# Attention over packed keys: the values as stationary operand for pair items and the latents' last four groups, with the even projections moved up and the output's addition ahead of a copy

## The chip, the cores and the metric

The kernel runs on one core of a Trainium2 chip. The metric is the device time of one launch in microseconds (us), as the median of several runs. TensorE does the matmuls; ScalarE, VectorE and GpSimd (POOL in the profile) do the rest; SyncE (SP) issues the loads.

## The reference, cut to what matters

Three stages follow each other on x of 4 batches x 256 rows x 256 columns. The change is in the first, a cross attention from the normed rows of x (the latents) to 4096 context tokens of the batch and the latents themselves, with a mask over the context:

```python
q = ln_lat @ Wq                                   # 16 heads of 64
kv = jnp.concatenate([xn, ln_lat], axis=1) @ Wkv
k, v = jnp.split(kv, 2, axis=-1)
weight = jnp.einsum('bhld,bhnd->bhln', q * scale, k * scale)
weight = jnp.where(full_mask[:, None, None, :], weight, neg)
weight = jax.nn.softmax(weight, axis=-1)
out = jnp.einsum('bhln,bhnd->bhld', weight, v)    # 256 queries, n keys, 64 columns a head
x = x + out.transpose(0, 2, 1, 3).reshape(b, l, heads * dim_head) @ Wout
```

The other two stages (a causal attention and two layers of local attention with a feed forward part) are not touched.

## The kernel before, in words

`cross_stage` (lines 103 to 1021) handles the keys of a batch in **items**. The chunks of 128 keys that the mask leaves are listed on the chip, and an item is `latents` (the 256 latents as keys), `pair` (two listed chunks, 256 keys) or `half` (one chunk, 128 keys). `walk` (line 141) gives each engine the same order: the latents of a batch, its pairs, its half, then the next batch. The softmax is an online one: a running maximum `mstate`, a factor `alpha` for what is summed so far, and the sum `o` of 32 columns groups of 64 values and one sum of weights each (65 columns; `v` carries a column of ones, so that the sum of weights comes out of the same matmul).

An item has 8 **steps** j = 0 to 7, one for each group g of 2 heads x 2 query tiles (4 units u of 128 queries). Each engine writes its own order out by hand in its `body` and waits on semaphores. In step j, TensorE (line 371) does:

- in an even step of pair and half items, the scores of groups j and j + 1 (`scores`, line 269). They are split products in fp32r, and head 0 and head 1 lie on partitions 0 to 63 and 64 to 127, so on two row halves of the array;
- the transposes of the probabilities of group j - 2 (`turn_probs`, line 283), 8 for 256 keys;
- one projection of the item's keys or values, or of the next item's first keys in steps 6 and 7 (`projections`, line 322), into the one bank `proj`;
- the weighted values of group j - 3 (`weighted_values`, line 294), plain f32 matmuls: the turned probabilities `pt` are stationary (128 x 128) and 65 columns of `v` move, 8 matmuls for 256 keys, into the bank `pv_ps`;
- in step 3, the next item's tokens turned (`turn_tokens`, line 246).

Groups 5 to 7 of an item thus have their weighted values in steps 0 to 2 of the next item, and the transposes of 6 and 7 stand in its steps 0 and 1.

VectorE (line 842) does in step j: the addition `o += pv_ps` of group j - 4 (`add_output`, line 814); in step 4 the next tokens times the norm's gain (line 753); the maxima of group j (`maxima`, line 786), which also copy the scores out of PSUM; the copy of half the transposes of j - 2 (`store_turned`, line 806; the other half is ScalarE's, line 514); and then one piece of other work: low parts of keys `kl` (line 766) in steps 0, 4, 6 and 7, statistics of the next tokens in step 0, the normed tokens `z` in step 2, the low part of the turned tokens in step 5, penalties in step 7.

ScalarE (line 539) does the copy of the transposes of j - 2, the copy of the projection (`kh` or `v`), then `softmax_part` (line 500): alpha and the exponentials of group j, 4 activations. POOL (line 660) multiplies `o` by alpha, group by group. SP loads tokens and masks for each item.

The next group's weighted values overwrite `pv_ps` and wait for `o_added` of the group ahead (line 299).

## Time and profile before

| | us |
|---|---|
| median of 3 runs | 1054.45 (1053.31 to 1056.25) |
| the profiled execution, its own time | 1054.65 |
| its span, first to last instruction | 1052.8 |
| TensorE busy (matmuls), ScalarE, VectorE, POOL | 1014.3, 666.8, 809.3, 204.1 |
| the cross stage, from the start to about | 662 |
| mean granted clock of TensorE | 0.995 |

A timeline row has the start in us from the span's start, how long the instruction (or, with a count xN, the run of N like it) took, the engine, the line, the operation, the written tile <- what it reads, and the shape. Matmuls overlap, so the distance between two starts is the time that one costs; 'took' is from its start to its result. A scores row "64*128 ... x2" is the two heads on the two row halves. A matmul on plain f32 appears as two instructions (two passes). "idle" in brackets is the time that the engine stood still before, with what ended it.

### The profile page before, as it was taken

The page shows a single profiled execution, that of the slowest core. Times are in us where ns is not written, and L with a number is a line of the kernel's source. Part 1 is how long each engine was busy: PE and PEld are TensorE (multiplying, and loading weights), DVE is VectorE, ACT ScalarE, POOL GpSimd, SP SyncE. Part 2 cuts the span into 40 slices and gives each one's busy share as a digit, 9 for nine tenths or more (in the row PEclk, how much of TensorE's full clock was granted, in tenths as well). Part 3 has the DMA queues.
Part 4 walks back from the last instruction along what each step waited for, and adds up shares of the span by engine and source line. Part 5 has one row for each costly group of instructions (what it writes and reads, how often), then busy time and mean ns, then how long its engine had stood idle before and what let it go on. Part 6 is the DMA issues. An engine that isn't in the chain of part 4 may idle for free. (4 is left out here: it accounts for less than half of the span.)

```text
span 1052.8 us, 25657 instructions
## 1 busy us (share of the span) xinstructions
PE 1014.3 (96%) x8683; PEld 943.1 (90%) x8684; DVE 809.3 (77%) x3001; ACT 666.8 (63%) x1550; POOL 204.1 (19%) x265
## 2 busy tenths in 40 slices
PE   6999999999999999999999998988999999999997
PEld 6899999999999999999999998977888999889887
DVE  7887777685877786787787777579879889889753
ACT  4765565674665665566565566478776876767753
POOL 0111111110111111111111111342015203263213
PEclk9999999999999999999999999999999999999999
DMA  6000000000000000000000100520010000110000
GB/s 208 18 13 2 10 1 1 12 12 4 12 2 0 12 13 3 13 2 0 12 13 2 35 2 2 166 38 2 1 41 21 2 1 21 35 48 2 1 22 21
DMA packets 28803, 21.64 MB, mean 21 GB/s; under 512 B 12094, under 2 KB 26267, under 8 KB 28699
## 3 DMA queue, kind: packets, MB, share of 16 engines
q1 hardware_dynamic: 28529, 20.21, 6.5%
q8 instruction: 62, 1.02, 0.4%
q14 instruction: 42, 0.34, 0.1%
q10 hardware_dynamic: 170, 0.07, 0.0%
HBM read 19.17 MB, written 1.05 MB: 19 GB/s over the span
## 5 line engine op out<-in xcount | busy, mean ns | idle before, releaser
L303 PEld LDWEIGHTS pv_ps<-v,pt 128*128 128x128 f32 x1792 | 214.9, 192 | 9.3 <-issue 2.8
L303 PE MATMUL pv_ps<-v,pt 128*128 128x65 f32 x1792 | 215.2, 272 | 3.2 <-DVE o L818 1.8
L796 DVE CUSTOM_DVE_ANT_0 s_sb<-s_ps,pen,mstate 128x256 f32<-128x256 f32 (+1 forms) x512 | 199.9, 446 | 13.9 <-issue 11.0
L510 ACT ACTIVATE probs<-s_sb,mbias 128x256 f32<-128x256 f32 (+1 forms) x512 | 203.2, 470 | 0.0
L670 POOL TENSOR_TENSOR o<-o,alpha 128x260 f32<-128x260 f32 x128 | 85.7, 669 | 561.3 <-ACT alpha L504 561.3
L519 ACT ACTIVATE pt<-turn 128x512 f32<-128x512 f32 x128 | 76.2, 595 | 123.0 <-PE turn L290 109.1
L290 PE MATMUL turn<-ident,probs 128*128 128x128 f32 x896 | 123.8, 278 | 0.1
L290 PEld LDWEIGHTS turn<-ident,probs 128*128 128x128 f32 x896 | 98.8, 145 | 9.5 <-issue 0.3
L818 DVE TENSOR_TENSOR o<-o,pv_ps 128x260 f32<-128x260 f32 x128 | 53.9, 421 | 46.1 <-PE pv_ps L303 34.7
L279 PE MATMUL s_ps<-kh,qh 64*128 64x256 f32 (+1 forms) x512 | 78.9, 304 | 2.9 <-DVE x L840 1.6
L768 DVE TENSOR_TENSOR kl<-proj,kh 128x512 fp32r<-128x512 f32 (+1 forms) x63 | 41.3, 655 | 51.5 <-ACT kh L497 51.0
L497 ACT ACTIVATE kh<-proj 128x512 fp32r<-128x512 f32 (+1 forms) x63 | 35.9, 570 | 65.2 <-PE proj L66 64.8
L64 PE MATMUL proj<-xt_hi,wkv_hi 128*128 128x256 f32 (+1 forms) x252 | 75.8, 301 | 0.0
L279 PE MATMUL s_ps<-kl,qh 64*128 64x256 f32 (+1 forms) x512 | 71.6, 275 | 0.0
L279 PE MATMUL s_ps<-kh,ql 64*128 64x256 f32 (+1 forms) x512 | 71.4, 275 | 0.0
L66 PE MATMUL proj<-xt_hi,wkv_lo 128*128 128x256 f32 (+1 forms) x252 | 71.3, 283 | 0.0
L65 PE MATMUL proj<-xt_lo,wkv_hi 128*128 128x256 f32 (+1 forms) x252 | 71.0, 282 | 0.0
L1251 POOL TENSOR_TENSOR late_lo<-f_hidden,late_hi 128x256 fp32r<-128x256 f32 x48 | 37.3, 781 | 162.8 <-ACT late_hi L1848 162.8
L1802 ACT ACTIVATE f_p<-f_p,f_bias,f_q_norm 128x128 f32<-128x128 f32 (+1 forms) x128 | 62.0, 540 | 5.9 <-DVE f_bias L2106 5.8
L812 DVE COPY pt<-turn 128x512 f32<-128x512 f32 x92 | 63.6, 692 | 1.9 <-issue 1.9
L279 PEld LDWEIGHTS s_ps<-kh,qh 64*128 64x128 f32 x512 | 48.4, 185 | 10.5 <-issue 5.0
L64 PE MATMUL f_g<-f_xm_hi,f_w_hi 128*128 128x256 f32 x192 | 54.7, 285 | 2.2 <-issue 2.2
(432 smaller groups left out, 2730.7 us busy)
## 6 DMA issues: line engine op xcount, KB each, us to landing
raw<-in_ctx SPq DMA_DIRECT2D x24, 128.0 KB, 2.0
f_wqkv_raw<-in_L_ffn_wqkv SPq DMA_DIRECT2D x6, 512.0 KB, 5.3
f_w_raw<-in_L_ffn_w SPq DMA_DIRECT2D x8, 256.0 KB, 5.1
f_w_raw<-in_L_ffn_w SPq DMA_DIRECT2D x2, 640.0 KB
wkv_raw<-in_L_xattn_Wkv SPq DMA_DIRECT2D x1, 1024.0 KB, 8.5
wout_raw<-in_L_xattn_Wout SPq DMA_DIRECT2D x1, 1024.0 KB, 12.5
f_wo_raw<-in_L_ffn_wo SPq DMA_DIRECT2D x2, 512.0 KB, 4.7
x<-in_x SPq DMA_DIRECT2D x1, 768.0 KB, 9.6
```

Of the source, the lines that this page charges most:

```text
L64: pe.matmul(out, s_hi, m_hi, start=first, stop=False)
L65: pe.matmul(out, s_hi, m_lo, start=False, stop=False)
L66: return pe.matmul(out, s_lo, m_hi, start=False, stop=last)
L279: last = pe.matmul(t.s_ps[g % 2][:, QT * o + qt, 0:width], q[rows, g, qt * P:(qt + 1) * P], k[rows, g, 0:width], start=first, stop=end)
L290: last = pe.transpose(bank[:, (at * kts + kt) * P:(at * kts + kt + 1) * P], t.probs[g % 2][:, u, kt * P:(kt + 1) * P], t.ident[:])
L303: last = pe.matmul(t.pv_ps[:, u, :], t.pt[g % 2][:, u, kt, :], t.v[:, kt, h, :], start=(kt == 0), stop=(kt == kts - 1))
L510: last = act.activation(t.probs[g % 2][:, u, 0:kts * P], t.s_sb[g % 2][:, u, 0:kts * P], ACT.Exp, bias=t.mbias[:, at:at + 1], scale=0.125)
L519: act.activation(t.pt[g % 2][:, 0:count, 0:kts, :], t.turn[0][:].rearrange("p (u k q) -> p u k q", u=count, k=kts), ACT.Copy).then_inc(s[" ...
L670: pool.tensor_tensor(t.o[:, cols, :], t.o[:, cols, :], t.alpha[:, cols].unsqueeze(2).broadcast_to([P, GU, DH + 1]), ALU.mult).then_inc(s[" ...
L796: last = dve.tensor_tensor_reduce(out=t.s_sb[g % 2][:, u, 0:width], in0=t.s_ps[g % 2][:, u, 0:width], in1=t.pen[:, 0:width], scale=1.0, sc ...
L812: dve.tensor_copy(t.pt[g % 2][:, 2:4, :, :].rearrange("p u k q -> p (u k q)"), t.turn[1][:]).then_inc(s["pt_ready"], 1)
L1802: last = act.activation(t.p[(2 * at + o) % 4][:, cols], t.p[(2 * at + o) % 4][:, cols], ACT.Exp, bias=t.bias[:, p % 2, q, o:o + 1], scale= ...
```

## The change

1. **Values as weights.** For all groups of pair items and for groups 4 to 7 of latents items (`turned`), `v` becomes stationary (128 keys x 64 columns, a head) and `pt` moves (2 query tiles, 256 columns). Head 0 writes partitions 0 to 63 of `pv_ps`, head 1 partitions 64 to 127; group g takes half g % 2 of the bank. The result is transposed, so for two groups together ScalarE copies the bank to `ov` (`store_outputs`), TensorE transposes it back into `pv_ps` (`turn_back`, 4 transposes, in odd steps) and VectorE adds 512 columns (`add_pair`).
2. **Sums.** The column of ones in `v` is gone. The exponentials write their sums (`accum_out`), and POOL adds them to `o` in an instruction of its own behind the multiplication.
3. **Order.** In even steps of pairs (0, 2, 4) and in steps 0 and 2 of halves, the projection stands right behind the scores, ahead of the transposes. In all even steps of pairs and in those steps of halves the weighted values stand right behind the transposes. ScalarE's copy of the transposes and `store_outputs` follow the projection's copy. On VectorE `add_pair` stands behind the maxima and ahead of the copy of the transposes, and `kl` of steps 0 and 4 ahead of that copy.
4. In the opening two semaphores are merged into others, and two planning tiles lie in `onorm`, for space.

```diff
+    def early(kind, prev, j):
+        return j % 2 == 0 and (kind == "pair" or kind == "half" and j < 4)
+    def turned(kind, prev, j):
+        owner, g = (kind, j) if j >= 0 else (prev, j + NG)
+        return owner == "pair" or owner == "latents" and g >= 4
+    def pair_told(kind, g):
+        return 7 if kind == "half" and g == NG - 1 else 1
+    def pair_at(m, kind, prev, j):
+        return at_step(m, kind, prev, j - 4) if j % 2 and turned(kind, prev, j - 4) else None
...
-            def weighted_values(m, g, kts):
+            def weighted_values(m, g, kts, transposed):
                 pe.wait_ge(s["pt_ready"], 16 * m + 2 * g + 2)
                 if g % 4 == 0:
                     pe.wait_ge(s["v_ready"], 4 * m + g // 2 + 2)
-                if g or not isinstance(m, int):
+                if (not transposed or g % 2 == 0) and (g or not isinstance(m, int)):
                     pe.wait_ge(s["o_added"], 8 * m + g)
...
+                for kt in range(kts if transposed else 0):
+                    for o, rows in enumerate((slice(0, DH), slice(DH, P))):
+                        last = pe.matmul(t.pv_ps[rows, g % 2, :], t.v[:, kt, 2 * g + o, :], t.pt[g % 2][:, QT * o:QT * o + QT, kt, :],
+                                         start=(kt == 0), stop=(kt == kts - 1))
                 last.then_inc(s["pv_done"], 1)
+            def turn_back(m, g, told):
+                pe.wait_ge(s["ov_stored"], 4 * m + g // 2 - 1)
+                for k in range(2):
+                    for qt in range(QT):
+                        last = pe.transpose(t.pv_ps[:, qt, k * P:(k + 1) * P], t.ov[:, k, qt * P:(qt + 1) * P], t.ident[:])
+                last.then_inc(s["o_turned_back"], told)
...
+                    if early(kind, prev, j) and j < 6:
+                        projections(m, b, kind, j, final)
                     now = at_step(m, kind, prev, j - 2)
                     if now:
                         turn_probs(*now)
+                    pair = pair_at(m, kind, prev, j)
+                    if pair:
+                        turn_back(pair[0], pair[1], pair_told(kind, pair[1]))
+                    now = at_step(m, kind, prev, j - 3)
+                    if now and early(kind, prev, j):
+                        weighted_values(*now, turned(kind, prev, j - 3))
...
-                                          bias=t.mbias[:, at:at + 1], scale=0.125)
+                                          bias=t.mbias[:, at:at + 1], scale=0.125, accum_out=t.sums[:, at:at + 1])
...
+            def store_outputs(m, g, told):
+                act.wait_ge(s["pv_done"], 8 * m + g + 1)
+                act.activation(t.ov[:], t.pv_ps[:], ACT.Copy).then_inc(s["ov_stored"], told)
...
+                    pool.wait_ge(s["rescaled"], 16 * m + 2 * g + 1)
+                    pool.wait_ge(s["p_ready"], 8 * m + g + 1)
+                    pool.tensor_tensor(t.o[:, cols, DH], t.o[:, cols, DH], t.sums[:, cols], ALU.add).then_inc(s["rescaled"], 1)
...
-            dve.memset(t.v[:, :, :, DH:DH + 1], 1.0).then_inc(s["x_added"], 2)
...
+            def add_pair(m, g, kts):
+                cols = slice(GU * (g - 1), GU * (g + 1))
+                dve.wait_ge(s["o_turned_back"], 4 * m + g // 2 - 1)
+                dve.wait_ge(s["rescaled"], 16 * m + 2 * g + 1)
+                added = t.o[:, cols, 0:DH].rearrange("p (h q) d -> p h q d", q=QT)
+                dve.tensor_tensor(added, added, t.pv_ps[:].rearrange("p q (h d) -> p h q d", d=DH), ALU.add).then_inc(s["o_added"], 2)
...
                         maxima(m, j, KINDS[kind])
+                    if early(kind, prev, j) and j in (0, 4):
+                        keys_lo(m, 2 + j // 4, KINDS[kind] * P)
+                    pair = pair_at(m, kind, prev, j)
+                    if pair:
+                        add_pair(*pair)
                     now = at_step(m, kind, prev, j - 2)
                     if now:
                         store_turned(*now)
...
-            t.v = sb("v", [P, KT, H, DH + 1])
+            t.v = sb("v", [P, KT, H, DH])
+            t.ov = sb("ov", [P, 2, L])
...
+            t.key_row = t.onorm[:, 0, 0:P]
+            t.below = t.onorm[:, 1, 0:P].rearrange("p (b c) -> p b c", b=B)
...
-            t.pv_ps = ctx.enter_context(nc.psum_tensor("pv_ps", [P, GU, DH + 1], F32))
+            t.pv_ps = ctx.enter_context(nc.psum_tensor("pv_ps", [P, 2, L], F32))
```

## Rows read from the trace of the kernel before

**Rows 1.** Busy time by stretch: one pair item; the stage. Columns: stretch, us, busy of each (count), clock.

```profile
98.11:137.76 39.65, 39.65 (x365) 37.67 (x364) 30.91 (x128) 24.03 (x60) 5.29 (x8) 1.00 0.03 7
...
0.00:662.00 662.00, 646.09 (x5842) 609.90 (x5844) 508.37 (x2137) 402.68 (x1008) 87.73 (x134) 1.00 0.05 16
```

**Rows 2.** Waits: TensorE, first 662 us. Columns: total us, times, longest.

```profile
PE pv_ps L303 <- DVE o L818: 1.8, 5, 0.8
```

**Rows 3.** Timeline of TensorE in that item and into the next.

```profile
107.91 0.39 PE L279 MATMUL s_ps<-kh,qh 64*128 64x256 f32 x2
...
117.59 0.61 PE L250 MATMUL proj<-ident,z 128*128 128x128 f32 x4
118.13 0.38 PE L279 MATMUL s_ps<-kh,qh 64*128 64x256 f32 x2
...
127.93 0.39 PE L279 MATMUL s_ps<-kh,qh 64*128 64x256 f32 x2
...
128.28 0.28 PE L279 MATMUL s_ps<-kh,ql 64*128 64x256 f32 x2
...
129.32 0.28 PE L279 MATMUL s_ps<-kh,ql 64*128 64x256 f32 x2
129.54 1.09 PE L290 MATMUL turn<-ident,probs 128*128 128x128 f32 x8
130.38 0.36 PE L64 MATMUL proj<-xt_hi,wkv_hi 128*128 128x256 f32 x1
...
131.89 1.89 PE L303 MATMUL pv_ps<-v,pt 128*128 128x65 f32 x16
133.62 1.04 PE L290 MATMUL turn<-ident,probs 128*128 128x128 f32 x8
134.42 0.36 PE L64 MATMUL proj<-xt_hi,wkv_hi 128*128 128x256 f32 x1
...
135.94 1.90 PE L303 MATMUL pv_ps<-v,pt 128*128 128x65 f32 x16
137.76 0.39 PE L279 MATMUL s_ps<-kh,qh 64*128 64x256 f32 x2
```

**Rows 4.** The page's costliest groups: VectorE's copy of the transposes.

```profile
L812 DVE COPY pt<-turn 128x512 f32<-128x512 f32 x92 | 63.6, 692 | 1.9 <-issue 1.9
```

**Rows 5.** Timeline of TensorE: two f32 matmuls of 256 columns in the next stage.

```profile
680.89 0.59 PE L1480 MATMUL f_pv<-raw,f_pt 128*128 128x256 f32 x2
681.32 0.59 PE L1481 MATMUL f_pv<-raw,f_pt 128*128 128x256 f32 x2
```

**Rows 6.** Timeline of VectorE, under rows 3 and in the items beside.

```profile
111.64 0.73 DVE L749 TENSOR_SCALAR z<-raw,mv,rstd 128x256 f32<-128x256 f32 x2
...
132.72 0.69 DVE L768 TENSOR_TENSOR kl<-proj,kh 128x512 fp32r<-128x512 f32 x1 [0.98 <-ACT kh L497]
...
134.17 0.48 DVE L796 CUSTOM_DVE_ANT_0 s_sb<-s_ps,pen,mstate 128x256 f32<-128x256 f32 x1
...
136.27 0.69 DVE L812 COPY pt<-turn 128x512 f32<-128x512 f32 x1
...
143.17 0.42 DVE L736 BATCH_NORM_STATS2 stats<-raw 128x6 f32<-128x256 f32 x1
...
144.12 0.42 DVE L818 TENSOR_TENSOR o<-o,pv_ps 128x260 f32<-128x260 f32 x1
```

**Rows 7.** Timeline of ScalarE in the same double step.

```profile
130.66 0.60 ACT L519 ACTIVATE pt<-turn 128x512 f32<-128x512 f32 x1 [1.55 <-PE turn L290]
132.09 0.60 ACT L497 ACTIVATE kh<-proj 128x512 fp32r<-128x512 f32 x1 [0.83 <-PE proj L66]
```

**Rows 8.** Timeline of ScalarE: exponentials without a sum, and with one (next stage).

```profile
127.41 1.70 ACT L510 ACTIVATE probs<-s_sb,mbias 128x256 f32<-128x256 f32 x4
...
675.59 0.51 ACT L1877 ACTIVATE f_gelu<-f_gelu,f_mid_bias 128x256 f32<-128x256 f32 x1
...
676.10 0.49 ACT L1877 ACTIVATE f_gelu<-f_gelu,f_mid_bias 128x256 f32<-128x256 f32 x1
```

More of the change, by code:

```diff
@@ L297, in weighted_values @@
                     pe.wait_ge(s["v_ready"], 4 * m + g // 2 + 2)
-                if g or not isinstance(m, int):
+                if (not transposed or g % 2 == 0) and (g or not isinstance(m, int)):
                     pe.wait_ge(s["o_added"], 8 * m + g)
-                for u in range(GU):
-                    h = 2 * g + u // QT
+                for u in range(0 if transposed else GU):
                     for kt in range(kts):
-                        last = pe.matmul(t.pv_ps[:, u, :], t.pt[g % 2][:, u, kt, :], t.v[:, kt, h, :],
+                        last = pe.matmul(t.pv_ps[:, g % 2, u * DH:(u + 1) * DH], t.pt[g % 2][:, u, kt, :], t.v[:, kt, 2 * g + u // QT, :],
+                                         start=(kt == 0), stop=(kt == kts - 1))
+                for kt in range(kts if transposed else 0):
+                    for o, rows in enumerate((slice(0, DH), slice(DH, P))):
+                        last = pe.matmul(t.pv_ps[rows, g % 2, :], t.v[:, kt, 2 * g + o, :], t.pt[g % 2][:, QT * o:QT * o + QT, kt, :],
                                          start=(kt == 0), stop=(kt == kts - 1))
                 last.then_inc(s["pv_done"], 1)
+            def turn_back(m, g, told):
[4 more added lines that the diff above has]
+                last.then_inc(s["o_turned_back"], told)
             def turn_output(b, u):
@@ L430, in body @@
                         output_projection(b, 1)
-                    if kind:
+                    if kind and not (early(kind, prev, j) and j < 6):
                         projections(m, b, kind, j, final)
@@ L439, in body @@
                         pe.wait_ge(s["plan_rows"], 1)
-                    if now:
-                        weighted_values(*now)
+                    if now and not early(kind, prev, j):
+                        weighted_values(*now, turned(kind, prev, j - 3))
                     if kind and j == 3 and not final:
@@ L465, in _ @@
             project_keys(0, KB)
-            pe.wait_ge(s["keys_spread"], 1)
-            pe.matmul(t.pv_ps[0:B, 1, 0:NCH + 1], t.row_of[:], t.listed[:], start=True, stop=True).then_inc(s["keys_listed"], 1)
+            pe.wait_ge(s["flags_ready"], 3)
+            pe.matmul(t.pv_ps[0:B, 1, 0:NCH + 1], t.row_of[:], t.listed[:], start=True, stop=True).then_inc(s["flags_ranked"], 1)
             pe.wait_ge(s["w_lo"], 3)
@@ L542, in body @@
                     now = at_step(m, kind, prev, j - 2)
-                    if now:
+                    if now and not (early(kind, prev, j) and j < 6):
                         store_turned(*now)
+                    last = at_step(m, kind, prev, j - 3) if turned(kind, prev, j - 3) else None
+                    if last and early(kind, prev, j) and j == 6:
+                        store_outputs(last[0], last[1], pair_told(kind, last[1]))
                     if finish and j in (1, 2, 4, 5):
                         store_output(b, {1: 0, 2: 1, 4: 2, 5: 3}[j], kind)
+                    if last and kind is None and j % 2 == 0:
+                        store_outputs(last[0], last[1], pair_told(kind, last[1]))
                     if final and j == 2:
@@ L594, in body @@
                             query_hi(0, 2 + j, True)
+                        if now and early(kind, prev, j) and j < 6:
+                            store_turned(*now)
+                        if last and j % 2 == 0 and not (early(kind, prev, j) and j == 6):
+                            store_outputs(last[0], last[1], pair_told(kind, last[1]))
                         softmax_part(m, j, kts)
@@ L822, in normalise_output @@
                 dve.wait_ge(s["o_added"], 8 * m - 4 + 4 * half)
+                dve.wait_ge(s["rescaled"], 16 * m - 8 + 8 * half)
                 dve.reciprocal(t.inv[:, cols], t.o[:, cols, DH]).then_inc(s["inverse"], 1)
@@ L852, in body @@
                     now = at_step(m, kind, prev, j - 4)
-                    if now:
+                    if now and not turned(kind, prev, j - 4):
                         add_output(*now)
@@ L877, in body @@
                             weights_lo(range(6, 7))
-                        keys_lo(m, 2, KINDS[kind] * P)
+                        if not early(kind, prev, j):
+                            keys_lo(m, 2, KINDS[kind] * P)
                     elif j == 4:
-                        keys_lo(m, 3, KINDS[kind] * P)
+                        if not early(kind, prev, j):
+                            keys_lo(m, 3, KINDS[kind] * P)
                     elif j == 6 and not final:
@@ L2566, in program @@
             t.pt = [sb(f"pt{k}", [P, GU, KT, P]) for k in range(2)]
[L2567 to L2568 removed]
+            t.mstate, t.mnew, t.mdiff, t.mbias, t.alpha, t.inv, t.sums = (
+                sb(n, [P, H * QT]) for n in ("mstate", "mnew", "mdiff", "mbias", "alpha", "inv", "sums"))
             t.o = sb("o", [P, H * QT, DH + 1])
             t.onorm = sb("onorm", [P, QT, H * DH])
+            t.key_row = t.onorm[:, 0, 0:P]
+            t.below = t.onorm[:, 1, 0:P].rearrange("p (b c) -> p b c", b=B)
             t.ot, t.ot_raw = split("ot", [P, 8, L])
```

25 lines of the change are left out of this document (12 added, 13 removed).

## The prediction

> **What bounds the kernel now.** I read the busy table by stretch first, then TensorE's timeline of one pair item, then the other engines' timelines under it. One item of kind pair takes 39.65 us, and TensorE is busy in all of it, at a granted clock of 1.00; VectorE has 30.91 us of work in it and ScalarE 24.03 [rows 1]. Over the first 662 us TensorE is idle for only 16. So in this stage a us of TensorE's queue is a us of the result, as long as VectorE and ScalarE answer in time. They do: the weighted values wait for VectorE's addition for 1.8 us in all [rows 2]. What the reader has to see in the timeline is the double step, an even step and the odd one behind it, since the scores of two groups stand together [rows 3]: scores to 1.61, transposed probabilities to 2.45, projection to 3.96, weighted values to 5.69, then transposes to 6.49, projection to 8.01, weighted values, and the next scores at 9.83. The four double steps of an item take 9.80, 10.22 (it has the turned tokens), 9.80 and 9.83.
>
> **How many.** The copy of the second half of the transposes on VectorE runs 92 times [rows 4]; the opening's four groups have theirs on ScalarE, so 96 groups are two key tiles wide, 12 items: 4 of latents and 8 pairs. Turned are 8 x 8 + 4 x 4 = 80 of 128 groups.
>
> **Term 1, the weighted values.** Now a group is 8 matmuls, each in 2 passes of 65 columns, 16 weight loads of 128 columns: 1.73 us from 131.89 to 133.62 [rows 3]. After, it is 4 matmuls (2 key tiles, 2 heads), 8 passes of 256 columns. The trace has f32 matmuls of 256 columns against 128 columns of weights: the next one starts 0.43 us later, so 0.215 a pass [rows 5]. One after the other, 8 passes are 1.72 us: nothing gained. The two heads write partitions 0 to 63 and 64 to 127, with 64 columns of weights each, so they can run side by side. No row shows two column halves at once. The nearest are the scores, where the two heads lie on two row halves: nine pairs go by in 1.04 us, 0.116 a pair of 256 columns, which is what one alone takes [rows 3]. That is the lower bound, 4 x 0.215 = 0.86; the serial 1.72 is the upper. I take a value between: both passes of one matmul stand behind each other in the queue on the same half, so head 0's first pass runs alone, then its second beside head 1's first, and so on: 5 slots, 1.08 us.
>
> **Term 2, changing the shape of the array.** 12 pairs at 0.116 are 1.40, but the scores take 1.61 to the transposes, and 0.09 lie ahead of them (weighted values from 135.94 end 1.73 later, at 137.67; the scores start at 137.76 [rows 3]): 1.70, 0.30 over for two changes, 0.15 each. The turned weighted values add three changes a double step, 0.45. From nothing (no drain between column halves) to twice that are the bounds. The Trainium skill, "TensorEngine Tiling (Array Packing)", Key Properties, says a change of tiling mode drains TensorE, and that tiles run in parallel, up to 2x for 64 columns; read by its factor the block would be 0.86 and not 1.08, and that is a rival below.
>
> **Term 3, turning back.** 4 more transposes for two groups; 8 take 0.80 [rows 3], so 0.42 with its margin.
>
> **TensorE's own sum** of a double step: 1.61 + 1.51 + 0.80 + (0.30 + 1.08) + 0.80 + 0.42 + 1.52 + (0.15 + 1.08 + 0.09) = 9.36 against 9.83. If nothing else ended last, that is 0.47 x 4 = 1.9 us an item and 15 in all.
>
> **Term 4, what is late next.** The even groups' weighted values stand in the odd step, and they wait until the addition of the pair ahead has read the bank. That addition (512 elements from PSUM; the subtraction kl of that size takes 0.69 [rows 6]) is now in VectorE's queue behind the odd step's maxima, where the old additions stood ahead of them. The odd maxima in turn stand behind the even step's copy of the transposes, and these transposes come 1.51 later than now, because the projection goes in front. So there is a chain in every double step, from the scores' start at 0. Even transposes end at 1.61 + 1.51 + 0.80 = 3.92, seen by a copy 0.28 later [rows 3, 7], taken as 4.22 with slack. After a projection kh starts 0.20 later [rows 3, 7] and kl another 0.63 [rows 6, 7]; kl occupies 0.62, the copy as much. Maxima 2.10 (134.17 to 136.27), addition 0.69, then 0.15 + 1.08 + 0.09.
> First double step: projection ends 3.12, kl 3.95 to 4.57, copy to 5.19, the next item's statistics 0.95 (143.17 to 144.12 [rows 6]) to 6.14, maxima to 8.24, addition 8.93, scores at **10.25**. TensorE stands free at 8.04, so it waits 0.9.
> Second: copy 4.22 to 4.84, normalised tokens 0.73 [rows 6] to 5.57, maxima 7.67, addition 8.36, weighted values 9.59, turned tokens 0.54: **10.13**.
> Third: kl to 4.57, copy 5.19, maxima 7.29, addition 7.98, ahead of TensorE's 8.04: **9.36**.
> Fourth: here the projection stays late and the turned weighted values go ahead of it: transposes end 2.45, weighted values with changes 3.83, projection 5.34, kl 6.17 to 6.79, maxima 8.89, addition 9.58: **10.90**. Before the change this kl starts at 4.79 [rows 6], 1.4 earlier.
> Sum 40.64 against 39.65: 1.0 us an item more, **8 us for 8 items**. The gain of term 1 is eaten by the wait for the addition.
>
> **Edits taken at nothing, and their cover.** The sums in the exponentials: an accumulated one is followed by the next 0.51 later [rows 8] where without it four take 1.70, 0.40 from one to the next when the last one's own 0.5 is taken off; so 0.1 x 4 a group, and the copy ov 0.5 for two groups: ScalarE gets 8 x 0.4 + 4 x 0.5 = 5.2 us an item on the 24.0 of 39.65. A group's probabilities end near 8 in the step and are transposed past 13; if that cover goes, every group costs up to 0.4, 51 in all. The bank turned back waits for the copy ov: weighted values end 5.15, seen and copied by 5.95, while the transposes in front end 6.10: 0.15 to spare, and a miss would come ahead of a wait anyway. The extra addition on POOL (128x4) stands behind p_ready; POOL has 5 us of work in 40 [rows 1]. No DMA is added or moved; SP's queue is as it was. The plan's renamed waits, the memset of v and the aliases in onorm lie in the opening, under 1 us either way.
> **Half items and latents.** The last pair item's groups 5 to 7 fall into the half item; with its narrower maxima and kl the first double step gains about 0.4 and the second loses 0.3 by the terms above; the latents' step 7 gains 0.2 and each latents item pays for ScalarE's sums where it is full. I take all of it as +0 and keep 4 us to either side.
>
> **Forecast.** 1054.65 (profiled execution; span 1052.8, the median of three is 1054.45, so no shift between them) + 8 = 1062.5; the median after, **1062**. With the unknown latencies of term 4 at 0.1 to 0.2 us a double step, its own range is 1056 to 1070.
>
> **Rivals.**
> *Fully side by side.* The block is 0.86. Then 10.03, 9.91, 9.08 and 10.46 (two blocks in that chain) = 39.48, 0.2 less an item: 1054.65 - 1.4 = 1053. For it: the scores' pairs. Against: a matmul here is two passes, the scores' one. Decides at a block of about 0.90. With cheaper changes too it comes to some 1047.
> *Not slower, TensorE's sum holds.* If the addition arrives before TensorE's 8.04 in each double step (statistics, kl and copy shorter in the chain than I added, by 0.3 to 1.5), the item is 37.7: 1054.65 - 15 = 1039.5. For it: VectorE has 8.7 us idle an item. Against: the order of its queue, which is written out.
> *The halves do not run at once.* The change then does not do what it says: 8 passes in 1.72. The chains give 10.89, 10.77, 10.64 and 12.18 = 44.5, 4.8 an item, 39, and 0.64 a group for the three turned groups in each of 4 half items and the one in each of 4 latents items, 10: 1103. For it: no row shows column halves. Against: the row halves run so.
>
> **Numbers.** Forecast 0.43, fully side by side 0.21, TensorE's sum 0.18, serial 0.18. A measurement can tell 0.3%, 3.2 us. Faster: 0.18 and half of the second, 0.28. Same: the rest of the second and the low end of the first, 0.15. Slower 0.57. The range runs from the third case's end to the first's with the half and latents items' margins, 1036 to 1074, and leaves out the serial case.
>
> **What would show it.** Starts of the turned weighted values: two column halves within one 0.22 slot, 5 slots a group (1.08), or 4, or 8. In the waits, TensorE's weighted values for the pair's addition, 0.9 us in the first double step, 0.3 in the second and 1.2 in the fourth, none in the third: 20 us in all where there are 1.8. Pair items of 40.6 us. The prediction is wrong if that wait is small, or if TensorE is busy throughout and the item is over 42 us.

## The result and the profile after

| | before | after |
|---|---|---|
| median, us | 1054.8 in this comparison | **1076.4** (1070.4 to 1077.6, 4 runs) |
| ratio, 95% interval | | 1.0194 (1.0151 to 1.0236) |
| span of the profiled execution | 1052.8 | 1075.5 |
| TensorE, ScalarE, VectorE, POOL busy | 1014.3, 666.8, 809.3, 204.1 | 995.7, 730.1, 807.5, 232.3 |

The change makes the kernel slower, by 1.9% (interval 1.5 to 2.4%). That direction was the likeliest in the prediction, but the forecast was 1062, and the measured median lies 2.4 us above the range of 1036 to 1074. The same kernel measured again (c1) has 1073.2, just inside it.

Busy time by stretch of the kernel after: a pair item; a half item and the latents behind it; two stretches in the last batch's pair item; the stage. Columns as in [rows 1].

```profile
97.46:137.82 40.36, 37.25 (x318) 29.17 (x316) 30.42 (x126) 28.61 (x96) 6.90 (x16) 1.00 0.03 7
178.19:213.72 35.53, 34.71 (x323) 30.49 (x321) 24.71 (x124) 25.00 (x96) 7.10 (x17) 1.00 0.04 10
213.72:260.39 46.67, 44.91 (x389) 40.87 (x389) 36.24 (x138) 30.79 (x98) 8.11 (x15) 1.00 0.03 8
...
590.00:595.00 5.00, 3.95 (x22) 3.73 (x22) 1.50 (x9) 0.00 (x0) 0.00 (x0) 0.53 0.49 166
595.00:600.00 5.00, 5.00 (x32) 3.95 (x31) 3.69 (x16) 3.15 (x9) 0.62 (x1) 0.79 0.01 2
0.00:670.00 670.00, 617.33 (x5313) 518.92 (x5315) 498.11 (x2086) 463.35 (x1555) 116.42 (x262) 0.99 0.05 16
```

A pair item was 39.65 with TensorE busy throughout [rows 1]; now it is 40.36 and TensorE is busy for 37.25 of it. The work on TensorE did become less, by 2.4 us in this item. What it waits for stands in its waits, first 665 us (total, times, longest), where [rows 2] has 1.8 us:

```profile
PE pv_ps L323 <- DVE o L878: 26.1, 28, 2.1
...
PE turn L307 <- DVE pt L864: 4.0, 6, 1.1
PE s_ps L296 <- DVE x L901: 3.0, 3, 1.0
...
PE s_ps L296 <- issue: 2.5, 2, 2.2
```

The timeline of TensorE in the first double step of that item answers to [rows 3], and VectorE's under it to [rows 6]:

```profile
97.46 0.39 PE L296 MATMUL s_ps<-kh,qh 64*128 64x256 f32 x2
...
99.06 0.39 PE L64 MATMUL proj<-xt_hi,wkv_hi 128*128 128x256 f32 x1
...
100.60 1.03 PE L307 MATMUL turn<-ident,probs 128*128 128x128 f32 x8
101.56 1.08 PE L323 MATMUL pv_ps<-pt,v 128*64 128x256 f32 x8
102.77 1.09 PE L307 MATMUL turn<-ident,probs 128*128 128x128 f32 x8
...
106.70 1.08 PE L323 MATMUL pv_ps<-pt,v 128*64 128x256 f32 x8 [1.00 <-DVE o L878]
107.72 0.39 PE L296 MATMUL s_ps<-kh,qh 64*128 64x256 f32 x2
```

```profile
101.43 0.69 DVE L820 TENSOR_TENSOR kl<-proj,kh 128x512 fp32r<-128x512 f32 x1 [0.52 <-ACT kh L533]
102.04 0.68 DVE L864 COPY pt<-turn 128x512 f32<-128x512 f32 x1
102.64 0.42 DVE L788 BATCH_NORM_STATS2 stats<-raw 128x6 f32<-128x256 f32 x1
...
103.67 0.49 DVE L848 CUSTOM_DVE_ANT_0 s_sb<-s_ps,pen,mstate 128x256 f32<-128x256 f32 x1
...
105.96 0.69 DVE L878 TENSOR_TENSOR o<-o,pv_ps 128x512 f32<-128x512 f32 x1
```

This is the chain of term 4: kl, the late copy of the transposes, the next item's statistics, the maxima from 103.67, the addition at 105.96, and 1.00 us of TensorE idle in front of the second block of turned weighted values. A block takes 1.02 from its start to the next operation (106.70 to 107.72), change of shape included.

**Where the time went.** The starts of the scores in both timelines give the sum up to the last item of the stage. Opening: 2.3 us gained (the first pair item starts at 56.14 instead of 58.44; in c1 it starts at 56.93). Four pair items that follow another pair: 40.37 against 39.65, +2.9 in all. The first pair items of batches 0 to 2: 41.3, 41.1, 41.1 against 39.7, +4.5. The last batch's, which is its only one: 48.1 against 39.7, **+8.5**. Latents items: +1.4. Half items of batches 0 to 2: 0; the last one, up to its fourth group: +1.4. Together +16.3 at 659, where the last half's fourth group of scores starts. The other 6.4 come behind that point, 4.5 in a second profile of the same kernel (c1).

The 48.1 us item begins so (TensorE):

```profile
588.59 0.28 PE L296 MATMUL s_ps<-kl,qh 64*128 64x256 f32 x1
591.05 0.37 PE L296 MATMUL s_ps<-kl,qh 64*128 64x256 f32 x1 [2.19 <-issue]
...
591.43 0.41 PE L296 MATMUL s_ps<-kh,qh 64*128 64x256 f32 x2
591.65 0.41 PE L296 MATMUL s_ps<-kl,qh 64*128 64x256 f32 x2
```

In the middle of a run of scores, with nothing that releases it, TensorE stands for 2.19 us. Then its pairs come 0.21 apart instead of 0.12: the granted clock is 0.53 from 590 to 595 and 0.79 to 600 (the rows above), so for some us it stands at 1.2 instead of 2.4 GHz. Before, this item had no stop and 9.81 us for its first double step; here it takes 15.00.

Two more things make this item long. VectorE too stops with nothing that releases it, for 1.39 us in the middle of the maxima of the second double step:

```profile
608.08 0.48 DVE L848 CUSTOM_DVE_ANT_0 s_sb<-s_ps,pen,mstate 128x256 f32<-128x256 f32 x1
...
609.96 0.08 DVE L848 DVE_READ_ACCUMULATOR2_ANT mnew<- 128x1 f32 x1 [1.39 <-issue]
```

The addition stands behind these maxima, so TensorE waits 2.06 us for it where it waits 0.52 in the other items, and this double step takes 11.75 instead of 10.14. The third takes 10.71 instead of 9.32: after the wait of 2.06 the granted clock is 0.57 from 614 to 618. Every kernel here with the values as weights has this stop of VectorE, at the same place and 1.1 to 1.4 us long; the kernel before, c4, d1 and e1 have none.

The 1.4 us of the last half item are the chain of term 4 once more: VectorE's statistics for the next stage, some 2.5 us, stand there in front of the maxima and the addition, and TensorE waits 1.87 for it.

### The profile page after: what moved, and what is told of

The parts are those of the page before. It is cut to its first block and busy times, and to the rows that moved or that the text cites. A ratio compares the mean times of both kernels' runs of the same rounds, so it can differ in the third digit from the quotient of the medians.

```text
span 1075.5 us, 25611 instructions
## 1 busy us (share of the span) xinstructions
PE 995.7 (93%) x8203; PEld 861.5 (80%) x8204; DVE 807.5 (75%) x2960; ACT 730.1 (68%) x2102; POOL 232.3 (22%) x393
## 5 line engine op out<-in xcount | busy, mean ns | idle before, releaser
L546 ACT ACTIVATE probs<-s_sb,mbias 128x256 f32<-128x256 f32 (+1 forms) x512 | 238.9, 470 | 0.0
L323 PE MATMUL pv_ps<-pt,v 128*64 128x256 f32 x640 | 86.9, 391 | 26.5 <-DVE o L878 26.1
L546 ACT ACTIVATION_READ_ACCUMULATOR probs<-s_sb,mbias 128x1 f32 x512 | 97.0, 190 | 0.0
L820 DVE TENSOR_TENSOR kl<-proj,kh 128x512 fp32r<-128x512 f32 (+1 forms) x63 | 41.3, 656 | 62.6 <-ACT kh L533 62.1
L323 PEld LDWEIGHTS pv_ps<-pt,v 128*64 128x64 f32 x640 | 40.9, 136 | 57.4 <-issue 24.0
L319 PEld LDWEIGHTS pv_ps<-v,pt 128*128 128x128 f32 x512 | 62.1, 191 | 7.6 <-issue 6.2
L319 PE MATMUL pv_ps<-v,pt 128*128 128x64 f32 x512 | 63.2, 271 | 3.8 <-DVE o L871 3.8
```

The lines of the kernel that those rows point to most:

```text
L319: last = pe.matmul(t.pv_ps[:, g % 2, u * DH:(u + 1) * DH], t.pt[g % 2][:, u, kt, :], t.v[:, kt, 2 * g + u // QT, :], start=(kt == 0), stop ...
L323: last = pe.matmul(t.pv_ps[rows, g % 2, :], t.v[:, kt, 2 * g + o, :], t.pt[g % 2][:, QT * o:QT * o + QT, kt, :], start=(kt == 0), stop=(kt ...
L546: last = act.activation(t.probs[g % 2][:, u, 0:kts * P], t.s_sb[g % 2][:, u, 0:kts * P], ACT.Exp, bias=t.mbias[:, at:at + 1], scale=0.125, ...
```

## The experiments

The kernel before ran beside each group: 1055.1, 1054.9 and 1054.9 us. Double steps are read from the starts of the scores in TensorE's timeline.

### c1: the changed kernel again

No edit.

> The changed kernel once more, unchanged, for what of its 22 us belongs to the kernel and what to one execution. In the first profile the pair items take 40.36 us against 39.65, 5.7 for eight, and TensorE waits 26 us for the pair's addition; but 8 us come in one item at 587 us, where TensorE stood still in the middle of the scores for 2.2 us and its granted clock then fell to half, and 6 more come behind the stage, where no line is changed. Theory 1 (the addition's place in VectorE's queue is the cause of all): the time repeats within 2 us and the item at 587 is again 8 us too long. Theory 2 (stops of TensorE that set the clock back, which differ between executions): the pair items are 40.4 again to 0.1, but the item at 587 or the part behind the stage differs by over 3 us, and runs with a mean clock of 0.995 or more are 5 us or more below the others.

Measured: 1073.2 us (1069.9 to 1078.2), ratio 1.0176 (1.0151 to 1.02). The double steps of a pair item are 10.27, 10.17, 9.32, 10.66, as in the first profile (10.26, 10.14, 9.32, 10.65). The stop is there again, at the same matmul:

```profile
591.63 0.28 PE L296 MATMUL s_ps<-kl,qh 64*128 64x256 f32 x1 [1.92 <-issue]
```

So the stop belongs to the kernel and not to one execution. Its price varies: this last pair item has double steps of 13.78, 11.46, 9.31 and 10.65, together 45.2 us, 5.5 more than before and not 8.5, and behind the wait in its second double step the clock stays at 1.00. Neither theory fits in full: the stop repeats, but item and time are 3 us shorter. In the next stage this execution has a granted clock of 1.00 from 700 to 850, where the first profile had 0.94; the 2 us more that the first profile loses behind the stage go with it.

### c2: the late loads held

```diff
+            sp.wait_ge(s["k_ready"], 61)
             for k, name in enumerate("QKV"):
                 sp.dma_start(t.late_raw[:, KC * k:KC * k + KC, :], ...)
```

> The three loads of the next stage's weights (768 KB) wait until the last pair item is nearly done (about 620 us); in the changed kernel they go out at 588.7 us, just as TensorE stops inside the scores. Theory 2a (TensorE's instructions come late behind those loads): the stop at the start of the last pair item is gone, its double steps are 10.9, 10.1, 9.3 and 10.7, the following half's 9.2, and the time falls by 6 to 9 us where the stop and the low clock were. Theory 1 and the view that the stop comes from the wait for x alone: no change within 2 us.

Measured: 1075.7 us, ratio 1.0193 (1.018 to 1.0206). The last pair item has double steps of 14.27, 11.41, 9.31, 10.64 and the stop stays at that matmul:

```profile
593.98 0.28 PE L297 MATMUL s_ps<-kl,qh 64*128 64x256 f32 x1 [2.47 <-issue]
```

The profiled execution is the slowest of the six (1083.9; the others lie between 1074.7 and 1076.4). The three loads that SP issues there do not cause the stop. That theory falls. All of the item is 2.7 us later here than in the first profile, and the stop keeps its place in the scores.

### c3: a shorter chain on VectorE

In pair and half items the next item's statistics go from step 0 to behind the addition in step 1, and step 6 of pairs gets the early projection, kl and copies too.

```diff
-                    if early(kind, prev, j) and j < 6:
+                    if early(kind, prev, j):
                         projections(m, b, kind, j, final)
...
-                    if j == (2 if prev is None else 0):
+                    if j == (2 if prev is None else 0 if kind == "latents" else 1):
```

> The chain from the scores to the pair's addition is made shorter in two places of pair items, nothing else is changed: the statistics of the next tokens go behind the addition in the odd step (0.95 us out of the first double step's chain), and in step 6 the projection, its kl and ScalarE's copies take the early places that they have in steps 0, 2 and 4 (1.3 us out of the fourth's). Theory 1: double steps of 9.3, 10.1, 9.3 and 9.3, pair items of 38.1 us, 2.2 less each, 18 us in all, so 1054 to 1059; the wait for the addition falls from 26 us to under 8. Rival (TensorE's own queue with its switches or ScalarE sets the item): double steps stay over 10.0 and the gain is under 5 us.

Measured: **1052.7 us** (1046.3 to 1058.4, 12 runs), ratio 0.998 (0.9961 to 0.9998). Double steps 9.22, 10.13, 9.31, 9.22, so 37.9 an item, and the wait for the addition:

```profile
PE pv_ps L323 <- DVE o L878: 7.3, 9, 1.9
```

20 us go with two moves that leave all the work in place. The first double step loses 1.04 (the statistics were 0.95), the fourth 1.4. The chain through the addition is shown as what kept the change from gaining. The seven pair items of batches 0 to 2 give 17 of the 20 us. The last item still begins with 14.06, with TensorE's stop at the same matmul, though all is 17 us earlier.

### c4: the sums alone

Nothing is turned and nothing is early; the accumulated sums, POOL's second instruction and the 64-column values stay.

```diff
     def turned(kind, prev, j):
-        owner, g = (kind, j) if j >= 0 else (prev, j + NG)
-        return owner == "pair" or owner == "latents" and g >= 4
+        return False
```

and `early` returns False as well.

> Values not turned and nothing early; of the change only the sums by the exponentials with POOL's second instruction, 64 instead of 65 columns, the merged semaphores and the aliases remain. If ScalarE's 0.1 us an exponential is hidden, as the prediction has it: 1054.8, within 3 us, pair items 39.7 and latents items 46.3. Rival (ScalarE or POOL sets the latents and half items): latents items 47 or more and half items 36 or more, 1058 to 1065.

Measured: 1060.3 us, ratio 1.005 (1.0037 to 1.0063): outside the 1054.8 within 3 that was expected. Pair items 39.67 (9.81, 10.20, 9.81, 9.85), half items 35.6: there the sums are hidden. They are not in the latents items, 47.04 against 46.29 (2.2 us in three of them), as the rival had it for these:

```profile
211.87:258.91 47.04, 45.62 (x397) 42.17 (x397) 36.23 (x138) 31.16 (x99) 8.12 (x15) 1.00 0.03 8
```

No stop in the last pair item (9.81). Against the kernel before it is 1.9 us behind at 657, and 4.9 at 690: three us are lost in 30, in code that nobody touched.

### d1: the order alone

`turned` returns False, `early` stays.

> The changed kernel with its reordering (part 3) and its sums (part 2), but with no group turned: the weighted values stay 8 matmuls with 64 columns of v moving, the addition stays ahead of the maxima, nothing is copied to ov or turned back. Theory 1 (what makes a double step long is the pair's addition behind the maxima and behind the late copy of the transposes): here no weighted values wait for an addition behind maxima, so TensorE's own sum holds, double steps of 9.8 to 9.9 and 10.2, pair items of 39.7 us, and the time is that of the kernel with sums alone, 1060, within 3. Rival 2 (moving the projection ahead of the transposes costs by itself, since every copy behind it comes 1.5 us later): pair items of 40.2 or more and 1065 or more. Theory 3 (the stop in the last batch's first pair item hangs on where TensorE's code lies) says nothing of this kernel beforehand: its code is longer than the changed kernel's; if it stops in the scores of that item too, 5 to 8 us come on top.

Measured: 1068.1 us, ratio 1.0127 (1.011 to 1.0144): the rival's side. Three double steps are as expected (9.84, 10.25, 9.84), the fourth is 10.71 instead of 9.85. Its TensorE:

```profile
129.66 1.09 PE L306 MATMUL turn<-ident,probs 128*128 128x128 f32 x8
130.59 1.90 PE L318 MATMUL pv_ps<-v,pt 128*128 128x64 f32 x16
132.29 0.37 PE L64 MATMUL proj<-xt_hi,wkv_hi 128*128 128x256 f32 x1
...
135.39 0.39 PE L64 MATMUL proj<-xt_hi,wkv_hi 128*128 128x256 f32 x1 [0.54 <-DVE kl L819]
```

In step 6 the weighted values moved ahead of the projection, but the projection did not move. It starts at 132.29, 4.24 into the double step, where it stood at 2.45 before [rows 3]; its kl is as much later, and step 7's projection waits for it (0.54 idle; from the start of the transposes to the projection it is 1.57 instead of 0.80). With nothing turned this costs 0.87 x 8 = 7 us. With the values as weights it costs more: 10.66 with this order, 9.43 without it (d2).

### d2: the values as weights alone

`early` returns False, `turned` stays.

> The changed kernel with the values as weights (part 1) and the sums, and the pair's addition behind the maxima, but with TensorE's projection, ScalarE's copies and VectorE's kl in their old places in even steps. Theory 1: the copy of the even transposes now ends 1.1 us earlier, so the odd maxima and the addition come earlier wherever kl is not the last in the chain: double steps of about 10.5, 9.9, 9.5, 9.5, a pair item of 39.4 us where the changed kernel has 40.4; 1 us for each of 8 items and the first items of a batch, so 8 to 11 us under the changed kernel, 1063 to 1067 with the stop in the last item, 1056 to 1060 without. Rival (the early projection helped, as the change has it): the item is 40.4 or longer and the time 1073 or more.

Measured: **1062.7 us**, ratio 1.0063 (1.0042 to 1.0083). Double steps 10.49, 9.51, 9.55, 9.43 (the second was expected at 9.9): 39.0 an item, 1.4 less than with the reordering. The wait for the addition is 19.6 us, nearly all of it in the first double step behind the statistics. The rival (the early projection helped) falls. In the second double step TensorE stands nowhere, so its own sum can be read off:

```profile
107.14 0.38 PE L296 MATMUL s_ps<-kh,qh 64*128 64x256 f32 x2
...
108.75 1.09 PE L307 MATMUL turn<-ident,probs 128*128 128x128 f32 x8
109.59 0.48 PE L64 MATMUL proj<-wkv_hi,xt_hi 128*128 128x512 f32 x1
...
111.17 1.08 PE L323 MATMUL pv_ps<-pt,v 128*64 128x256 f32 x8
112.19 1.09 PE L307 MATMUL turn<-ident,probs 128*128 128x128 f32 x8
113.12 0.60 PE L332 MATMUL pv_ps<-ident,ov 128*128 128x128 f32 x4
113.47 0.48 PE L64 MATMUL proj<-wkv_hi,xt_hi 128*128 128x512 f32 x1
...
115.05 1.08 PE L323 MATMUL pv_ps<-pt,v 128*64 128x256 f32 x8
116.07 0.66 PE L267 MATMUL proj<-ident,z 128*128 128x128 f32 x4
116.65 0.38 PE L296 MATMUL s_ps<-kh,qh 64*128 64x256 f32 x2
```

From 107.14 to 116.07 are 8.93 us without the turned tokens; before, the same double step has 9.68 (107.91 to 117.59 [rows 3]). The last pair item starts with 14.41 here too, with the same stop, and takes 43.9 in all.

### d3: POOL held in the next stage

The lost us of c4 have a place. VectorE's two multiplications in the next stage's opening, from the timelines of before and of after, with POOL's instructions beside the second:

```profile
686.99 1.52 DVE L2282 TENSOR_SCALAR raw<-x,f_mv_first,f_rstd 128x256 f32<-128x256 f32 x2
```

```profile
702.34 3.62 DVE L2350 TENSOR_SCALAR raw<-x,f_mv_first,f_rstd 128x256 f32<-128x256 f32 x2
```

```profile
702.15 2.39 POOL L1174 TENSOR_TENSOR f_wo_lo<-f_wo_raw,f_wo_hi 128x1024 fp32r<-128x1024 f32 x1
704.50 2.59 POOL L1174 TENSOR_TENSOR f_w_lo<-f_w_raw,f_w_hi 128x512 fp32r<-128x512 f32 x2
```

The first multiplication ends at 704.69, 0.15 behind `f_wo_lo`, and the second at 705.96, 0.15 behind the first `f_w_lo` (705.81).

The edit makes POOL wait for the two ahead of `f_wo_lo`:

```diff
                     tables(0)
+                    pool.wait_ge(s["y_ready"], 2)
```

> The changed kernel, and in the next stage GpSimd begins the low part of wo only when VectorE has written the first two normed tiles (one more wait). Every kernel with the change so far showed VectorE's two multiplications there 3.65 us long from start to end where the kernel before has 1.52, and GpSimd's 2.4 us subtraction beside them. Theory L (VectorE's two stand still while GpSimd's long one runs): they take 0.8 to 1.0 us, TensorE's wait behind them goes, and 2 to 3 us of the 17 by which the changed kernel is later than the one before disappear: 1070.5 to 1072.5 against 1073 to 1076. Rival (they are long for another reason, the weights' loads or the clock): still 3.6 us, and the time the same or up to 1 us more for the later low parts.

Measured: 1070.6 us (1069.5 to 1074.5), ratio 1.0145 (1.0128 to 1.0162).

```profile
706.21 0.73 DVE L2351 TENSOR_SCALAR raw<-x,f_mv_first,f_rstd 128x256 f32<-128x256 f32 x2
...
707.07 2.38 POOL L1174 TENSOR_TENSOR f_wo_lo<-f_wo_raw,f_wo_hi 128x1024 fp32r<-128x1024 f32 x1 [0.98 <-issue]
```

0.73 for the two instead of 3.62, and the distance to the kernel before hardly grows over these us (19.2 at 657, 19.5 at 753; in the first profile, without the hold, 15.3 at 657 and 18.4 at 730), so theory L is shown. The Trainium skill, "SBUF — State Buffer", SBUF: two separate sides, calls the port pair of VectorE and GpSimd an exclusive lock held for a whole instruction; these runs agree: each multiplication ends just behind a whole GpSimd instruction, and the two lose 2.9 us. In the kernel before POOL was later at this place: it began its third `f_wqkv_lo` only 2.94 us after the second:

```profile
685.47 2.42 POOL L1106 TENSOR_TENSOR f_wqkv_lo<-f_wqkv_raw,f_wqkv_hi 128x1024 fp32r<-128x1024 f32 x1 [2.94 <-ACT f_wo_hi L1097]
```

In all kernels with the change the three stand back to back, and without the hold `f_wo_lo` meets the multiplications (3.6 to 3.7 us for the two, 7.6 in c2's profile). The trace puts the end of the pause down to ScalarE here and to nothing in e1 (2.74), so why POOL paused stays open.

### d4: TensorE's code moved by 96 waits

```diff
             turn_tokens(0)
+            for _ in range(96):
+                pe.wait_ge(s["state_set"], 1)
             pe.wait_ge(s["x_ready"], 1)
```

> The changed kernel with 96 more waits that are already met in TensorE's opening, ahead of its first projections, where it idles: nothing but the place of all later code is moved. Theory 3 (the stop of TensorE inside the scores of the last batch's first pair item, 1.9 to 2.5 us, hangs on where its code lies): the stop is gone or stands at another instruction of the item; if gone, the granted clock stays at 1.00, the item's first double step is 10.9 to 11.5 instead of 13.8 to 15.0 and the time 4 to 7 us less, 1067 to 1071. Rival 3b (it hangs on something in the work, such as the loads or the other engines): the stop is at the same matmul with the same 1.9 to 2.5 us, and the time is the changed kernel's, 1073 to 1076, or up to 3 more for the waits in the opening.

Measured: 1078.0 us (1072.2 to 1083.3), ratio 1.0229 (1.0178 to 1.028), so the time is a miss. In the profiled execution (1074.3) the last pair item has 10.26 for its first double step and 41.7 in all: TensorE's stop is gone from there. VectorE's, whose code did not move, is not (1.12). TensorE stops now at the entries of the pair items of batches 1 and 2, where it only waited 1.0 for x in the changed kernel:

```profile
264.48 0.39 PE L296 MATMUL s_ps<-kh,qh 64*128 64x256 f32 x2 [3.30 <-issue]
```

and 2.45 us at 430.29. Each contains that wait, so these items begin 2.3 and 1.4 us later than in the changed kernel. Nothing but the place of the code differs, and about 1 us in the opening; c2 and c3 moved the item by 2.7 and 17 us, and the stop kept its place. So theory 3 is shown in that the stop hangs on where TensorE's code lies. The hope of a cure is not: two of the four executions took 1082 and 1083 us at a mean granted clock of 0.986, and no profile shows where.

### e1: the kernel before, its code moved

The same 96 waits in the kernel before.

> The kernel before, with 96 waits that are already met in TensorE's opening: its later code only stands elsewhere. Theory 3 (TensorE stops for 2 to 3 us where its code happens to cross some boundary at the entry of a loop; the kernel before had the luck to have none): here one to three stops of TensorE without a releaser appear inside the scores of an item that begins a loop, and the time rises by 2 to 8 us to 1057 to 1063. Rival 3b (only the changed kernel's code can stop): no stop, and 1055 to 1056, the waits in the opening adding at most 1.

Measured: 1056.5 us, ratio 1.0018 (1.0002 to 1.0033). One stop of 0.5 us at the entry of the first pair item, where the kernel before has one of 0.4; all items as they were. At this one other place of its code the kernel before has no stop of 1 us or more either, so theory 3's expectation missed, and what makes the changed kernel's code prone to it stays open.

### e2: the shorter chain, POOL held, 96 waits

> The short chain (statistics behind the addition, step 6's projection ahead of the transposes too), GpSimd's hold in the next stage and the 96 waits together. If the three are separate terms: 1052.7 - 2.5 for the hold, and the pad moves TensorE's stops from the last batch to the middle ones, between -4 and +3: 1046 to 1053. Double steps 9.2, 10.1, 9.3, 9.2 as in the short chain alone. Rival (gains in the stage are given back in the next one, which ends with other waits): 1052 to 1055 again.

Measured: 1056.9 us (1052.3 to 1062.3, 10 runs), ratio 1.0014 (0.9992 to 1.0036): a miss. The steady double steps are as expected and the multiplications at 0.73. TensorE's stops:

```profile
PE s_ps L296 <- issue: 6.8, 3, 3.3
```

This contains the waits of 1.0 for x at the entries of batches 1 and 2. The opening is no longer than in c3 (first pair item at 57.35 against 57.54). Against c3's profile the two entries cost 2.2 each and the first double steps behind them 0.8 each, 6.1 in all, and the last pair item gains 4.8. The last half item loses 3.2 up to its fourth group: the granted clock is 0.70 there from 627 to 636, and 1.00 in c3. The profiles of c2, d2 and d3 have such a low clock at the same place too. So the moved stops cost more than they save, by 1.3 us, and most of this profile's loss comes with the low clock in the last half.

### e3: step 2 in the old order

c3 and d3's hold, and

```diff
-        return j % 2 == 0 and (kind == "pair" or kind == "half" and j < 4)
+        return j % 2 == 0 and (kind == "pair" and j != 2 or kind == "half" and j == 0)
```

> The short chain and GpSimd's hold, with the early projection and weighted values in steps 0, 4 and 6 of pairs and step 0 of halves, and step 2 in the old order (the kernel with the old order in all steps showed 9.51 for the second double step where the early order has 10.14). Theory 1: in the second double step the turned tokens wait for nothing and the copy of the transposes no longer ends last: 9.22, 9.5, 9.3, 9.2, an item of 37.3 us, 0.6 under the short chain's 37.9: 1052.7 - 5 - 2.5 = 1045, 1043 to 1048. Rival (the order of step 2 only matters with the statistics in the chain): second double step over 10.0 and 1049 to 1051.

Measured: **1046.1 us** (1041.3 to 1047.9), ratio 0.9917 (0.9893 to 0.994). Double steps 9.22, 9.51, 9.32, 9.22, TensorE busy for 36.85 of 37.27:

```profile
95.94:133.21 37.27, 36.85 (x319) 28.86 (x318) 30.81 (x125) 28.51 (x96) 6.89 (x17) 1.00 0.03 8
```

Item and time are as expected. Against c3, 0.6 us an item come from step 2's order, and the hold in the next stage gives about 3: the early projection in step 2 was a loss by itself. By the working of term 4 the reason is that the copy of the transposes and the normalised tokens then end later and hold back the maxima that the addition waits behind; that is argued, no run takes it apart.

### e4: the same, with 48 waits

> The kernel with the mixed order and 48 waits already met in TensorE's opening. Theory 3 (stops hang on the place of the code): the stops of TensorE stand at other instructions than in the kernel without these waits and with 96, the items' double steps stay the same to 0.03 us elsewhere, and the time lies within 6 us of it on either side. Rival 3b: stops at the same matmuls, same time within 1 us.

Measured: **1043.0 us** (1041.6 to 1047.6), ratio 0.9891 (0.9858 to 0.9924), with the same double steps. The stop has moved to an earlier matmul of the last item's scores and is shorter; the item's first double step is 12.15 instead of 13.03:

```profile
566.50 0.38 PE L296 MATMUL s_ps<-kh,ql 64*128 64x256 f32 x2 [1.16 <-issue]
```

Theory 3 is confirmed once more, rival 3b falls. This is the fastest version, 1.1% under the kernel before, with the change's values as weights, its sums and most of its order; its interval overlaps that of e3.

## Why the prediction was right or wrong

- **Term 1.** The block is 1.02 us with its change of shape, so the halves run fully side by side: 4 slots of 0.215 are 0.86. In d2's trace the passes of the two heads start within 0.01 us of each other (111.172 and 111.179, 111.439 and 111.445), and the next pair 0.215 later. I took 1.08, a stagger that does not exist. The lower bound was right.
- **Term 2.** After 1.08 and the changes I had 1.38 and 1.32 for two blocks, 2.70 in a double step; they are 2.04. For the changes 0.16 a block are left, and perhaps the 0.13 by which the transposes behind it are longer (0.93, not 0.80).
- **TensorE's own sum** was 9.36 by the prediction and is 8.93 in d2's second double step. Mis-sized by 0.43: 0.66 less in terms 1 and 2, 0.23 more in the projections and transposes. The saving there is 0.75 (9.68 before), not 0.47.
- **Term 4, the chain** is the right mechanism. Forecast 10.25, 10.13, 9.36, 10.90; measured 10.26, 10.14, 9.32, 10.65; waits for the pair's addition forecast at 20 us, measured 26.1 and 26.0, of which 2.7 in a steady item (0.9 + 0.3 + 1.2 = 2.4 forecast). c3 shows it by taking it away. It hit partly by two errors that cancel: the blocks in it were shorter, and the addition begins some 0.2 later than worked out (maxima at 103.67, addition at 105.96: 2.29, not 2.10).
- **The count of items.** "For 8 items" took the steady item for all. Four are like that and cost 0.7 each. In the three that follow latents VectorE comes out of the latents late (TensorE's transposes wait for its copy, up to 1.1) and they cost 1.4 to 1.7 each. Before, TensorE was the bound there and hid it. These seven cost 7.3 us where the forecast had 7.0: the number came out by luck, and the miss does not lie here.
- **The step that failed: what was not in the sum.** The first profile is 22.7 us longer, 14.7 more than forecast: 7.5 in the last batch's pair item, 6.4 behind 659, 1.4 in the latents, 1.4 in the last half item, 0.3 in the other seven pair items, less 2.3 gained in the opening. The largest is the last batch's pair item, 8.5 us alone in the first profile and 5.5 in c1, where the prediction had 1.0. It comes from a stop of TensorE that no semaphore explains, with the granted clock at half behind it, and a stop of VectorE in the addition's chain. With TensorE's stop gone (d4) the item is 41.7, 2.0 over before. The longest such stop in this stage in the trace of before is 0.4, and the prediction had no term or rival for it. c1 and d4 show that TensorE's stop is the kernel's and hangs on where its code lies. What makes the code stop there stays open.
- **"Edits taken at nothing".** The sums are hidden in pair and half items, as argued. "Half items and latents ... as +0" holds for the halves. The latents pay 0.6 to 0.9 each in c4, 2.2 us in three. The last half item was not +0 but +1.4, by the next stage's statistics in the chain. The sum also stopped at the stage's end: the next stage loses some 3 us because POOL and VectorE meet at another moment (c4, d3). The latents and this are about the 5.2 us by which c4 is slower.
- **The split of the change.** Sums alone 1060.3; with the values as weights 1062.7; with the order alone 1068.1; all of it 1073 to 1076. So, beyond the sums, the order costs 7.8 and the two together 13 to 16. The 2.4 of the values as weights lie within the intervals of the two runs, and they contain TensorE's stop: d2's last pair item is 43.9 where c4's is 39.7, while its four steady ones are 0.7 shorter each. The prediction had charged the fourth double step with a late kl (10.90), and that is what d1 shows; that this comes from the order, and without turning too, it did not say.
- **The rivals.** "Fully side by side" had the block right and the time wrong, since the chain and not the block set the item. "TensorE's sum holds" has an item of 37.7; e3 reaches 37.27, by the moves that its condition named (statistics, kl and copy out of the chain), but 1046 and not 1039.5. "Serial" falls: the block is 1.02 and not 1.72.

## What to carry to other kernels

When a change makes the bounding engine faster, write out the chain that takes its place and ask of each piece in it whether it must stand there: here 0.95 us of statistics in front of the addition and one projection behind the weighted values decided between 1073 and 1053. An order that is moved must be moved whole: the weighted values went ahead of the projection in step 6 while the projection stayed, and that cost 7 us with nothing turned and more with the rest. And price the first and the last turn of a loop and the stage behind it apart from the steady one; 20.8 us lay there, of a loss of 22.7 in all.

## What the runs showed of the hardware that was not expected

- Two column halves run fully at the same time even for plain f32 matmuls of two passes: a pair of passes every 0.215 us, four pairs in 1.02 us with the change of shape.
- TensorE can stop for 1.2 to 2.5 us inside a run of matmuls with nothing to wait for, and VectorE for 1.1 to 1.4 inside its maxima. 96 more instructions ahead moved TensorE's stop from one item to the entries of two others (3.3 and 2.45 us, 1.0 of each a wait for x); 48 moved it within its item (1.16 instead of 2.19). Behind a 2.19 us stop the granted clock was 0.53 for 5 us, with scores 0.21 apart instead of 0.12.
- The trace lists DMA transfers of the kind "instruction". One on queue q8 begins at 588.6, within 0.3 us of TensorE's stop, and one on q14 at 608.2, 0.3 ahead of VectorE's. The DMA view of the kernel after, 585 to 590 and 605 to 625, lists them (packets, MB, share of the engines; narrower windows give the starts):

```profile
q8 instruction: 1, 0.02, 1.4%
...
q14 instruction: 2, 0.02, 0.2%
```

  Each stop of TensorE or VectorE named here, of 1 us or more, has such a transfer in it or beginning less than 2 us ahead of it, and the 96 waits moved those of q8 and not those of q14. So it is likely that the engine waits for its instructions. It is not shown: most of these transfers pass without a stop, and the kernel before has one 0.9 us behind the entry of the same item, as the kernel after has, and goes on.
- Two GpSimd subtractions, of 2.39 and 1.3 us, made two VectorE multiplications that take 0.73 together last 3.62.
